# Twelve-layer latent transformer on one core: the second norm of layer 5 as one factor a token, the last quarter's turn moved behind the first products of nine layers, the last layer's mean by TensorE

## The chip, the cores and the metric

One core of one Trainium2 chip. The kernel is one program of about 71,000 instructions, with one instruction stream for each of TensorE (PE), VectorE (DVE), ScalarE (ACT), GpSimd (POOL) and SyncE (SP, which issues all DMAs). The metric is the device time of one execution in microseconds.

## The reference, cut to what matters

The state `x` is 64 batches x 32 tokens x 128 features (2048 tokens), all in fp32. Twelve layers follow each other, each of the form

```python
x = x + layer(_layernorm(x))      # _layernorm: (x - mean) / sqrt(var + 1e-5), no gain, no offset
```

The layers are: 1 cross attention with mask, 2 linear attention with an MLP, 3 a three-matrix network with binary weights, 4 cross attention with mask, 5 an attention within a batch, 6 a mixture of experts, 7 sigmoid cross attention, 8 latent attention, 9 a grouped expert network, 10 cross attention, 11 an attention with a sparse branch and an MLP, 12 a GRU over the 32 tokens followed by routing and experts. Only in layers 5 and 12 does the arithmetic change. Layer 5 gets `y = _layernorm(x)` and norms it again, this time with a gain and an offset:

```python
h = _layernorm(y) * norm_w + norm_b
q, k, v = split(h @ qkv_w.T + qkv_b)
att = (q @ k.T) * 128 ** -0.5            # no softmax, so no row maxima either
out = y + (att @ v) @ proj_w.T + proj_b  # and then x = x + out
```

Layer 12 starts its GRU from a mean over the tokens of a batch: `h0 = y.mean(axis=1) @ ctx_w.T + ctx_b`.

## The kernel before, in words

**State and tiles.** `X` holds the 2048 tokens as 16 tiles of 128 tokens (partitions) x 128 features, side by side in one 128x2048 buffer; `y` is its norm and `yT` the turned norm (features on the partitions), of the same size. Four tiles are a quarter. `stats`, `moments` (mean and variance of each token) and `rstd` belong to the program and outlive a layer.

**Layers and their order.** Each layer is a class with one method for each engine (`pe`, `act`, `dve`, `pool`, `sp`); each engine works through its method in program order. Between layers stands a barrier: every engine drains, raises `closed` (L3877, L3884, L3891, L3904) and waits until all four have. So a layer starts when its slowest engine is through with the one before. Weights of the next layer are loaded by SP while a layer runs. Nothing is planned at run time; the order is the order of the calls, and waits are on counting semaphores.

**The norm at a layer's head.** A layer norms the first three quarters of the next one while it ends (`next_statistics`, `next_root`, `next_rows`). The last quarter is left to the next layer's head: DVE takes statistics (L103, L106, L109), ACT the square root (L115), DVE the reciprocal and four rows (L121, L124). PE turns all four quarters with 16 transposes (`norm_pe`, L240) into PSUM banks 0 to 3, and ACT copies each bank to `yT` (`norm_act_yT`, L231; L3297 in layer 12, where the copy also reorders the tokens by time). ACT does the square root first and then the four copies. In most layers the first product waits for all four copies, that is for the last quarter. In layer 1 this stays as it is.

**Layer 3** (`L0Ffn`). DVE first does the norm, then maps the three binary matrices from 0/1 to -1/1 (L1715, three instructions), drains, and subtracts the halves of the first (L1718); PE starts its first products (L1676) when all that is done.

**Layers 4 and 10** (`HeadCrossAttention`). PE first folds the last context token (L821 to L828), then does the 16 transposes, then the queries of tile 0 (L880), keys and values of group 0 (L886 to L888), those of group 1, and scores (L899). DVE adds the bias to the queries (L1074, L1076), POOL spreads them over the heads (L1182), DVE builds `wo_heads` (L1022) right behind. The steady state that follows goes by groups of 32 tokens.

**Layer 5** (`L1Attention`). Four groups of 512 tokens go through a pipeline of steps: norm again on DVE (`own_norm`: statistics L279, L282, L285, root on ACT L298, reciprocal L309, rows L312, times gain L303, plus offset L305), transposes (L1800), copy (L1826), queries, keys and values (L1790, L1793), scores (L1782), apply (L1774), projection (L1766). DVE adds three things for each group: projection plus `y` (L1842), plus the offset of the projection (L1844), plus `X` (L1846). Behind the third group stand the rows of three quarters of the next norm. POOL has nothing to do.

**Layer 12** (`L3Ffn`). Behind the four copies DVE sums `yT` over the tokens (L3487) and scales (L3489); PE forms `h0` (L3324); then follow 32 steps of the GRU (L3349) and the experts.

## Time and profile before

| | us |
|---|---|
| median of 3 runs | 3074.31 (3073.43 to 3076.48) |
| the profiled execution | 3070.85 |
| its span, first to last instruction | 3069.1 |
| busy PE, DVE, ACT, POOL | 2812.5, 1702.2, 1319.7, 689.9 |

The chain that ended last is PE for 54% of the span, DVE 7%, POOL 4%, ACT 3%. The layers start at 0, 459.6, 739.7, 838.0, 1113.9, 1160.4, 1266.1, 1354.8, 1500.3, 1586.3, 1854.1 and 2021.4 us of the span. How to read it: every row gives a start or a count, a duration, the engine, the line of the kernel, and what is written from what; the bracket at the end of a row is the idle time of the engine before it and what ended that.

### The profile page before, as it was taken

To read this page: it belongs to the slowest core of one execution; us is meant where nothing else is said; L and a number is where in the kernel's file an instruction comes from. 1 tells how busy PE (TensorE), PEld (TensorE's weight loads), DVE (VectorE), ACT (ScalarE), POOL (GpSimd) and SP (SyncE) were. 2 spreads that over 40 slices of the span, in tenths; PEclk is the share of its full clock that TensorE was granted. 3 is DMA by queue.
4 is the path that set the end of the run, shared out by engine and by line. 5 is a ranking of instruction groups with operands and counts; after the bars stand their busy time and mean duration, and the time that the engine had idled before them with its cause. 6 is when DMAs were issued, how large, how long until landed. Compare 5 with 4: busy or idle time off the path is not lost.

```text
span 3069.1 us, 71179 instructions
## 1 busy us (share of the span) xinstructions
PE 2812.5 (92%) x27569; PEld 1813.6 (59%) x27569; DVE 1702.2 (55%) x5653; ACT 1319.7 (43%) x3579; POOL 689.9 (22%) x1524
## 2 busy tenths in 40 slices
PE   8999998997999978999689997779999999999898
PEld 7888885554567755665457775534444444444465
DVE  6777777674166677558746765842233232232544
ACT  4655555542278842348538883411111121121222
POOL 2444440000067720024116661100000000000000
PEclk9999999998999988888779998989999999999999
DMA  5111110000021100230011113040000000000000
GB/s 133 49 47 47 49 31 8 2 3 5 12 55 48 48 25 3 67 106 2 5 40 43 39 29 142 2 136 1 1 1 1 1 1 1 1 1 1 1 1 14
DMA packets 125910, 92.28 MB, mean 30 GB/s; under 512 B 41027, under 2 KB 122566, under 8 KB 124230
## 3 DMA queue, kind: packets, MB, share of 16 engines
q1 hardware_dynamic: 125574, 87.74, 10.1%
q8 instruction: 219, 3.59, 0.5%
q14 instruction: 117, 0.96, 0.1%
HBM read 84.02 MB, written 3.67 MB: 29 GB/s over the span
## 4 chain that ended last, share of the span: by engine, by line
PE 54%; DVE 7%; issue 5%; POOL 4%; ACT 3%; DVEq 2%; POOLq 2%; ACTq 0%
PE banks L3349 24%; POOL probs L1208 3%; PE banks L918 2%; PE banks L3768 2%; PE banks L3759 2%; PE banks L3757 2%; PE banks L1682 2%; PE banks L899 1%; POOLq L1209 1%; PE banks L927 1%; PE banks L886 1%; PE banks L3404 1%; PE banks L2301 1%; PE banks L3359 1%; PE banks L1924 1%
## 5 line engine op out<-in xcount | busy, mean ns | idle before, releaser
L1008 ACT ACTIVATE probs<-probs,nbias 128x257 f32<-128x257 f32 x512 | 254.7, 507 | 0.0
L1208 POOL TENSOR_SCALAR probs<-probs,rinv 128x257 f32<-128x257 f32 x512 | 237.9, 485 | 29.3 <-DVE rinv L1102 25.6
L3349 PE MATMUL banks<-Wz,hT 128*64 128x256 f32 x2048 | 226.4, 379 | 0.0
L3349 PE MATMUL banks<-Wn,hT 128*64 128x512 f32 x1024 | 225.4, 593 | 0.0
L3349 PE MATMUL banks<-Wr,hT 128*64 128x512 f32 x1024 | 225.2, 592 | 0.0
L3618 POOL COPY rb<-hT 128x512 f32<-128x512 f32 x32 | 35.8, 1119 | 801.3 <-ACT hT L3424 777.0
L3349 PEld LDWEIGHTS banks<-Wz,hT 128*64 128x64 f32 x2048 | 147.0, 137 | 87.7 <-issue 18.3
L3592 DVE TENSOR_TENSOR pr<-hb,banks 128x512 f32<-128x512 f32 x32 | 22.0, 688 | 298.3 <-PE banks L3404 298.3
L712 POOL TENSOR_SCALAR probs<-probs,rinv 128x257 f32<-128x257 f32 x256 | 120.6, 485 | 201.3 <-DVE rinv L652 200.7
L3349 PEld LDWEIGHTS banks<-Wr,hT 128*64 128x64 f32 x1024 | 73.5, 137 | 132.6 <-issue 128.0
L3349 PEld LDWEIGHTS banks<-Wn,hT 128*64 128x64 f32 x1024 | 70.9, 137 | 129.5 <-issue 129.5
L918 PE MATMUL banks<-ident,probs 128*128 128x128 f32 x1024 | 140.7, 281 | 4.1 <-POOLq L1209 2.7
L3479 ACT ACTIVATE sq<-banks 128x512 f32<-128x512 f32 x32 | 19.1, 598 | 284.0 <-DVE pr L3592 284.0
L485 PE MATMUL banks<-kvT,qh 128*128 128x257 f32 x512 | 133.8, 384 | 1.0 <-ACT bo_rows L545 1.0
L568 ACT ACTIVATE probs<-banks,nbias 128x257 f32<-128x257 f32 x256 | 119.6, 474 | 34.6 <-DVE rinv L652 31.1
L918 PEld LDWEIGHTS banks<-ident,probs 128*128 128x128 f32 x1024 | 110.3, 141 | 31.0 <-issue 22.7
L640 DVE SCALAR_TENSOR_TENSOR banks<-banks,r_all,keep 128x257 f32<-128x257 f32 x256 | 113.2, 485 | 12.2 <-PE banks L485 8.1
L643 DVE CUSTOM_DVE_ANT_0 banks<-banks,fill 128x257 f32<-128x257 f32 x256 | 105.3, 447 | 15.0 <-issue 0.5
L1091 DVE CUSTOM_DVE_ANT_0 probs<-banks,fill 128x257 f32<-128x257 f32 x256 | 93.2, 421 | 21.5 <-PE banks L907 21.5
L1091 DVE CUSTOM_DVE_ANT_0 probs<-banks,zeros 128x257 f32<-128x257 f32 x256 | 93.2, 421 | 15.1 <-PE banks L899 15.1
L1008 ACT ACTIVATION_READ_ACCUMULATOR probs<-probs,nbias 128x1 f32 x512 | 99.7, 195 | 0.0
L3457 ACT ACTIVATE h<-banks 128x512 f32<-128x512 f32 x72 | 42.7, 598 | 132.1 <-PE banks L3757 132.1
(632 smaller groups left out, 6399.2 us busy)
## 6 DMA issues: line engine op xcount, KB each, us to landing
kvT<-in_ctx_T SPq DMA_DIRECT2D x192, 128.5 KB
kv<-in_ctx SPq DMA_DIRECT2D x64, 128.0 KB
kv<-in_ctx SPq DMA_DIRECT2D x32, 256.0 KB
W<-in_L_ffn_W_T SPq DMA_DIRECT2D x2, 2048.0 KB
Wr<-in_L_ffn_w_hh_T SPq DMA_DIRECT2D x1, 4096.0 KB
Wn<-in_L_ffn_w_hh_T SPq DMA_DIRECT2D x1, 4096.0 KB
Wz<-in_L_ffn_w_hh_T SPq DMA_DIRECT2D x1, 4096.0 KB
v_last<-v_last SPq DMA_DIRECT2D x192, 8.0 KB, 1.6
```

The source lines that it names most:

```text
L485: e.matmul(self.bank[self.S_BANK + n][:, 0:CTX], self.qh[t % 2][:, (4 * b + n) * P:(4 * b + n + 1) * P], self.kvT[b][:, :], start=True, st ...
L568: e.activation(self.probs[v][:, j * CTX:(j + 1) * CTX], self.bank[self.S_BANK + 2 * z + j][:, 0:CTX], ACT.Exp, bias=self.nbias[v][:, j:j + ...
L640: e.scalar_tensor_tensor(s[j], s[j], self.r_all[t % 2][:, r:r + 1], keep, ALU.add, ALU.mult)
L643: e.tensor_tensor_reduce(s[j], s[j], fill, 1.0, -3.0e38, ALU.add, ALU.max, top[j])
L712: i = e.tensor_scalar(s, s, self.rinv[v][:, j:j + 1], 1.0, ALU.mult, ALU.mult)
L918: i = e.transpose(self.bank[self.T_BANK + c][:, r * P:(r + 1) * P], probs[:, r * CTX + c * P:r * CTX + (c + 1) * P], self.prog.ident[:, :])
L1008: i = e.activation(s, s, ACT.Exp, bias=self.nbias[v][:, r:r + 1], scale=self.scale, accum_out=self.rows_sum[v][:, r:r + 1])
L1091: i = e.tensor_tensor_reduce(self.probs[v][:, r * CTX:(r + 1) * CTX], self.bank[r][:, 0:CTX], add, 1.0, -3.0e38, ALU.add, ALU.max, self.ma ...
L1208: e.tensor_scalar(s, s, self.rinv[v][:, r:r + 1], 1.0, ALU.mult, ALU.mult)
L1682: i = e.matmul(self.bank[2 + c % 2][:, :], self.W[1][:, k * 512 + c * P:k * 512 + (c + 1) * P], h0[:, k * R4:(k + 1) * R4], start=k == 0, ...
L3349: mm = e.matmul(self.bank[b][hf * BATCH:(hf + 1) * BATCH, 0:n], lhs, rhs, start=start, stop=stop, tile_position=(0, hf * BATCH))
L3757: e.matmul(self.bank[c][:, :], self.gate[:, o:o + P], yT, start=True, stop=True).then_inc(self.gate_mm.up(), 1)
```

## The change

- `norm_pe` and `norm_act_yT` take a list of quarters, and a stage may name the banks of the turns (`TURN_BANKS`).
- In layers 2 to 4 and 6 to 12 PE turns three quarters (one in layers 4, 10 and 11, the next two a little later), starts the first products that need only those, and turns the last quarter behind some of them. ACT copies one to three quarters ahead of the square root.
- Layer 3: the signs come ahead of the norm on DVE, and the first products wait for the first matrix alone; the root moves to round 1, the last quarter's turn to round 2.
- Layers 4 and 10: DVE takes the first queries between statistics and rows; POOL no longer waits for the rows.
- Layer 5: the second norm becomes one factor a token (`again`). The mean of `y` is zero and its variance is var * rstd^2, so the factor is 1 / sqrt(var * rstd^2 + 1e-5), from numbers that the first norm left. The gain is folded into the weights (`qkvG`), the offset into the biases (three small products into bank 7). POOL scales the rows and adds `y` and the projection's offset to `X`; DVE is left with one sum for each group, and with one quarter of the next rows for each group from the second on.
- Layer 7: DVE takes statistics, then fills `of_batch`, then the rows, and only then copies the folded matrices (`fold_ready`); ACT runs a square root on a constant at the head, which loads its table.
- Layer 8, 9, 11: order at the head. In layer 11 the sigmoid of `lam` moves behind the first projections and two quarters.
- Layer 12: PE forms the sum over the tokens with 16 products of a tile of `y` with a 128x4 matrix of zeros and ones that POOL builds (`of_row`); DVE only scales.

```diff
@@ layer 2: L0Attention, pe and act
-        self.norm_pe(e)
+        self.norm_pe(e, (0, 1, 2))
         self.weights_wait(e)
         for c in range(self.C):
             self.features(e, 0, c)
+            if c == 1:
+                self.norm_pe(e, (3,))
...
+        self.norm_act_yT(e, (0, 1))
         self.norm_act_std(e)
-        self.norm_act_yT(e)
+        self.norm_act_yT(e, (2,))
...
@@ layer 3: L0Ffn, pe, act, dve
-        self.norm_pe(e)
+        self.norm_pe(e, (0, 1, 2))
         self.signs_ready.wait_ge(e, 1)
-        self.n_yT.wait_ge(e, 4)
...
+            if r == 2:
+                self.norm_pe(e, (3,))
             for c in range(FC):
+                self.n_yT.wait_ge(e, max(r, c % 2) + 1)
...
-        self.norm_act_std(e)
-        self.norm_act_yT(e)
-        self.signs_ready.wait_ge(e, 1)
+        self.norm_act_yT(e, (0, 1, 2))
+        self.weights_wait(e)
...
+            if r == 1:
+                self.norm_act_std(e)
+            if r == 2:
+                self.signs_ready.wait_ge(e, 3)
+                self.norm_act_yT(e, (3,))
@@ layers 4 and 10: HeadCrossAttention, pe
-        p.constants_made.wait_ge(e, 1)
+        self.norm_pe(e, (0,))
         self.weights_wait(e)
...
+        self.norm_pe(e, (1, 2))
+        self.x_free = None
+        self.n_yT.wait_ge(e, 1)
+        self.prep_act.wait_ge(e, 1)
+        self.project(e, 0)
...
+        self.keys_values(e, 0)
+        self.norm_pe(e, (3,))
         self.n_yT.wait_ge(e, 4)
-        self.project(e, 0)
-        self.keys_values(e, 0)
@@ layer 5: L1Attention
+    def again_dve(self, e, n):
+        p, at = self.prog, self.tiles_again(n)      # n = 0: tiles 0 to 11, n = 1: tiles 12 to 15
+        r, rstd = self.again[:, at], p.rstd[:, at]
+        var = p.moments[:, 2 * at.start:2 * at.stop].rearrange("p (t two) -> p t two", two=2)[:, :, 1]
+        e.tensor_tensor(r, rstd, rstd, ALU.mult)
+        e.drain()
+        e.tensor_tensor(r, r, var, ALU.mult)
+        e.drain()
+        e.tensor_scalar(r, r, 1e-5, None, ALU.add).then_inc(self.again_var.up(), 1)
...
-                y, x, t1 = p.y[:, g * R4:(g + 1) * R4], p.X[:, g * R4:(g + 1) * R4], self.t1[g % 2]
-                e.tensor_tensor(t1[:, :], self.bank[6][:, :], y, ALU.add).then_inc(self.y_added.up(), 1)
-                e.drain()
-                e.tensor_tensor(four(t1), four(t1), row4(self.bp), ALU.add)
-                e.drain()
-                e.tensor_tensor(x, x, t1[:, :], ALU.add)
+                x = p.X[:, g * R4:(g + 1) * R4]
+                self.x_offset.wait_ge(e, g + 1)
+                e.tensor_tensor(x, self.bank[6][:, :], x, ALU.add).then_inc(self.x_done.up(), 1)
                 e.drain()
                 if g < 3:
                     self.next_statistics(e, g)
-                if g == 2:
-                    for q in range(3):
-                        self.next_rows(e, q)
+                if g:
+                    self.next_rows(e, g - 1)
...
+    def pool(self, e):
+        p = self.prog
+        self.weights_wait(e)
+        e.tensor_scalar(self.qkvG[:, :], self.qkvT[:, :], self.gw[:, 0:1], 1.0, ALU.mult, ALU.mult).then_inc(self.gained.up(), 1)
+        self.norm_again(e, 0)
+        self.norm_again(e, 1)
+        p.rowed.wait_ge(e, NT * (self.index + 1))
+        for g in range(self.GROUPS):
+            if 2 <= g + 1 < self.GROUPS:
+                self.norm_again(e, g + 1)
+            x, y_bp = p.X[:, g * R4:(g + 1) * R4], self.y_bp[g % 2]
+            e.tensor_tensor(four(y_bp), p.y[:, g * R4:(g + 1) * R4].rearrange("p (t d) -> p t d", d=P), row4(self.bp), ALU.add)
+            e.drain()
+            e.tensor_tensor(x, x, y_bp[:, :], ALU.add).then_inc(self.x_offset.up(), 1)
+
+    def norm_again(self, e, g):
+        self.again_ready.wait_ge(e, 1 + g // 3)
+        self.h_turned.wait_ge(e, g - 1)
+        for t in range(4 * g, 4 * g + 4):
+            s = t % 4
+            i = e.tensor_scalar(self.hn[g % 2][:, s * P:(s + 1) * P], self.prog.y[:, t * P:(t + 1) * P], self.again[:, t:t + 1], 1.0, ALU.mult, ALU.mult)
+        i.then_inc(self.hn_ready.up(), 1)
@@ layer 6: L1Ffn, pe (layer 7 has the same with cg in place of Wr)
+            if t == 12:
+                self.norm_pe(e, (3,))
+            self.n_yT.wait_ge(e, t // 4 + 1)
             i = e.matmul(bank[6][:, t * E:(t + 1) * E], yT[:, t * P:(t + 1) * P], self.Wr[:, :], start=True, stop=True)
@@ layer 7: L2CrossAttention, act
+        e.activation(self.warm[:, :], self.prog.ones[:, 0:1], ACT.Sqrt)
+        self.norm_act_yT(e, (0, 1))
         self.norm_act_std(e)
-        self.norm_act_yT(e)
+        self.norm_act_yT(e, (2, 3))
@@ layer 12: L3Ffn, pe and dve
-        self.norm_pe(e)
+        self.norm_pe(e, (0, 1, 2))
+        self.of_row_made.wait_ge(e, 1)
+        for t in range(NT):
+            if t == 12:
+                self.norm_pe(e, (3,))
+            i = e.matmul(bank[4][:, BPT * t:BPT * (t + 1)], p.y[:, t * P:(t + 1) * P], self.of_row[:, :], start=True, stop=True)
+        i.then_inc(self.mean_mm.up(), 1)
...
-        self.n_yT.wait_ge(e, 4)
-        e.tensor_reduce(self.mean[:, :], p.yT[:, :].rearrange("p (t b) -> p b t", b=BATCH), AX.X, ALU.add)
-        e.drain()
-        e.tensor_scalar(self.mean[:, :], self.mean[:, :], 1.0 / SEQ, None, ALU.mult).then_inc(self.mean_ready.up(), 1)
+        self.mean_mm.wait_ge(e, 1)
+        e.tensor_scalar(self.mean[:, :], bank[4][:, 0:BATCH], 1.0 / SEQ, None, ALU.mult).then_inc(self.mean_ready.up(), 1)
```

## Rows read from the trace of the kernel before

**Rows 1.** Stretches by layer: us, busy PE, PEld, DVE, ACT, POOL, granted clock, DMA share.
```profile
1113.90:1160.40 46.50, 29.33 (x160) 22.59 (x160) 40.10 (x145) 11.17 (x24) 0.04 (x1) 0.76 0.14 34
2021.40:3069.10 1047.70, 1023.38 (x6274) 487.99 (x6274) 358.27 (x732) 195.88 (x364) 40.26 (x55) 0.99 0.04 12
```
**Rows 2.** Groups by line in layer 5: shapes, count, busy us, mean ns, idle.
```profile
L312 DVE TENSOR_SCALAR hn<-y,mv,rstd 128x128 f32<-128x128 f32 x16 | 4.5, 342 | 0.3
L305 DVE TENSOR_TENSOR hn<-hn,gb 128x512 f32<-128x512 f32 x4 | 2.8, 692 | 0.3
```
**Rows 3.** Groups by line of POOL, whole span.
```profile
L1208 POOL TENSOR_SCALAR probs<-probs,rinv 128x257 f32<-128x257 f32 x512 | 237.9, 485 | 29.3 <-DVE rinv L1102 25.6 <-issue 2.5
L1182 POOL TENSOR_TENSOR qbd<-q,of_group 128x512 f32<-128x512 f32 x32 | 37.2, 1163 | 85.8 <-DVE q L1076 51.0 <-DVE q L1074 34.8
L1186 POOL COPY kT<-k_last 128x1 f32<-128x1 f32 x128 | 24.0, 188 | 12.4 <-PE banks L907 7.2 <-PE banks L899 5.2
L1642 POOL TENSOR_TENSOR y_bo<-y,bo 128x512 f32<-128x512 f32 x4 | 5.1, 1266 | 128.9 <-DVE s L1629 126.1 <-DVE y L124 2.8
```
**Rows 4.** Timeline of layer 5's head and of the next layer's first instruction: start, us, what.
```profile
1121.10 3.50 PE L1790 MATMUL banks<-hT,qkvT 128*128 128x512 f32 x4 [1.01 <-ACT hT L1826]
...
1160.43 4.17 PE L240 MATMUL banks<-ident,y 128*128 128x128 f32 x16 [5.83 <-DVEq L3891]
```
**Rows 5.** Timeline of POOL and DVE at layer 4's head.
```profile
844.88 2.28 DVE L1022 TENSOR_TENSOR wo_heads<-wo,head_mask 128x2048 f32<-128x2048 f32 x1
845.04 3.01 POOL L1182 TENSOR_TENSOR qbd<-q,of_group 128x512 f32<-128x512 f32 x1 [0.42 <-DVE q L1074]
```
**Rows 6.** Chain of waits at layer 3's head: start, us, what.
```profile
742.96 2.07 DVE W L1715 x3
745.18 0.69 DVE W L1718
745.96 6.75 PE banks L1676 x8
```
**Rows 7.** Timeline of layer 2's head.
```profile
459.59 1.53 PE L240 MATMUL banks<-ident,y 128*128 128x128 f32 x12 [0.99 <-POOLq L3904]
465.19 1.28 ACT L1510 ACT_TABLE_LOAD   x1 [1.32 <-PE banks L1360]
467.28 0.76 DVE L1589 TENSOR_SCALAR banks<-banks,bq 128x512 f32<-128x512 f32 x1 [4.35 <-ACT ex L1510]
```
**Rows 8.** Chain of waits in the heads of layers 4 and 10.
```profile
850.12 1.17 PE banks L899 x8
...
1594.01 2.95 POOL qbd L1182
1597.23 0.71 PE banks L899 x8
```
**Rows 9.** Chain of waits at the heads of layers 6, 7, 8 and 9.
```profile
1165.28 7.01 PE banks L1906 x32
...
1274.29 6.96 PE banks L2094 x32
...
1360.72 0.57 PE banks L2469 x2
...
1504.62 1.14 PE banks L3090 x2
```
**Rows 10.** Chain of waits at the heads of layers 11 and 12.
```profile
1863.53 1.89 PE banks L2301 x64
...
2023.37 3.53 ACT yT L3297 x4
2026.92 3.57 DVE mean L3487
2030.91 1.99 PE banks L3324 x4
```
**Rows 11.** The span and its mean granted clock.
```profile
core 0: 3069.1 us, clock 0.950
```

More of the change, by code:

```diff
@@ L199, in norm_dve, with own_quarters, norm_dve_statistics, norm_dve_rows @@
     def norm_dve(self, e):
-        quarters = range(3 if self.index else 0, 4)
+        self.norm_dve_statistics(e)
+        self.norm_dve_rows(e)
+    def own_quarters(self):
+        return range(3 if self.index else 0, 4)
+    def norm_dve_statistics(self, e):
         self.prog.x_loaded.wait_ge(e, 1)
-        for q in quarters:
+        for q in self.own_quarters():
             self.prog.norm_statistics(e, self.index, q)
-        for q in quarters:
+    def norm_dve_rows(self, e):
+        for q in self.own_quarters():
             self.prog.norm_rows(e, self.index, q)
@@ L225, in next_rows, with norm_act_yT, norm_pe @@
             self.prog.norm_rows(e, self.index + 1, q)
-    def norm_act_yT(self, e):
+    def norm_act_yT(self, e, quarters=range(4)):
         p = self.prog
-        for q in range(4):
+        for q in quarters:
             self.n_turned.wait_ge(e, q + 1)
-            e.copy(p.yT[:, q * 512:(q + 1) * 512], p.bank[q][:, :]).then_inc(self.n_yT.up(), 1)
-    def norm_pe(self, e):
+            e.copy(p.yT[:, q * 512:(q + 1) * 512], p.bank[self.TURN_BANKS[q]][:, :]).then_inc(self.n_yT.up(), 1)
+    def norm_pe(self, e, quarters=range(4)):
         p = self.prog
         p.constants_made.wait_ge(e, 1)
-        for q in range(4):
+        for q in quarters:
             for r in range(4):
@@ L1742, in __init__ @@
         self.bv, self.bp = self.broadcast_row("bv", w["qkv_b"][2 * P:3 * P]), self.broadcast_row("bp", w["proj_b"])
[L1743 removed]
+        self.gw, self.gb = self.columns("gw", w["norm_w"]), self.columns("gb", w["norm_b"])
         self.end_of_weights()
[L1745 removed]
+        self.same, self.qkvG = sb("same_batch", [P, P]), sb("qkvG", [P, 3 * P])
+        self.again = sb("again", [P, NT])
         two = lambda n: [sb(n, [P, R4]) for _ in range(2)]
[L1747 removed]
+        self.hn, self.hT, self.v, self.att, self.oT, self.y_bp, self.qT, self.kT = (two(n) for n in ("hn", "hT", "v", "att", "oT", "y_bp", "qT", "kT"))
         self.norm_signals(turned=False)
[L1749 removed]
+        self.gained, self.offset_mm, self.offset_ready = sig("gained", 1), sig("offset_mm", 1), sig("offset_ready", 1)
+        self.again_var, self.again_std, self.again_ready = sig("again_var", 2), sig("again_std", 2), sig("again_ready", 2)
         self.hn_ready, self.h_turned, self.hT_ready = sig("hn_ready", N), sig("h_turned", N), sig("hT_ready", N)
@@ L1759, in pe @@
         self.weights_wait(e)
+        for n in range(2):
+            e.matmul(bank[7][:, n:n + 1], self.qkvT[:, n * P:(n + 1) * P], self.gb[:, 0:1], start=True, stop=True)
+        e.matmul(bank[7][:, P:2 * P], self.gb[:, 0:1].to_broadcast([P, P]), self.qkvT[:, 2 * P:3 * P], start=True, stop=True).then_inc(self.offset_mm.up(), 1)
+        self.gained.wait_ge(e, 1)
         for step in range(N + 4):
@@ L1804, in act @@
         N = self.GROUPS
-        self.norm.act(e)
+        self.again_act(e, 0)
         self.norm_act_std(e)
+        self.again_act(e, 1)
+        self.offset_ready.wait_ge(e, 1)
         for step in range(N + 4):
@@ L1826, in act, with tiles_again, again_act, again_inverse @@
                 e.copy(self.hT[g % 2][:, :], self.bank[0][:, :]).then_inc(self.hT_ready.up(), 1)
-                if g + 1 < N:
-                    self.norm.act(e)
+    def tiles_again(self, n):
+        return slice(12 * n, 12 + 4 * n)
+    def again_act(self, e, n):
+        r = self.again[:, self.tiles_again(n)]
+        self.again_var.wait_ge(e, n + 1)
+        e.activation(r, r, ACT.Sqrt).then_inc(self.again_std.up(), 1)
+    def again_dve(self, e, n):
[7 more added lines that the diff above has]
+        e.tensor_scalar(r, r, 1e-5, None, ALU.add).then_inc(self.again_var.up(), 1)
+    def again_inverse(self, e, n):
+        r = self.again[:, self.tiles_again(n)]
+        self.again_std.wait_ge(e, n + 1)
+        e.reciprocal(r, r).then_inc(self.again_ready.up(), 1)
     def dve(self, e):
         p, N = self.prog, self.GROUPS
+        self.again_dve(e, 0)
+        self.norm_dve_statistics(e)
+        self.again_inverse(e, 0)
+        self.norm_dve_rows(e)
+        e.drain()
+        self.again_dve(e, 1)
         self.weights_wait(e)
-        self.own_norm(e, 0)
-        self.norm_dve(e)
+        self.offset_mm.wait_ge(e, 1)
+        e.tensor_tensor(self.bqk[:, :], self.bank[7][:, 0:2], self.bqk[:, :], ALU.add).then_inc(self.offset_ready.up(), 1)
+        e.tensor_tensor(self.bv[:, :], self.bank[7][:, P:2 * P], self.bv[:, :], ALU.add)
+        self.again_inverse(e, 1)
         same_batch(e, self.same, P ** -0.5)
@@ L3290, in tiles, with norm_act_yT @@
         return self.prog.X[t * BATCH:(t + 1) * BATCH, :].rearrange("b (j d) -> b j d", d=P)
-    def norm_act_yT(self, e):
+    def norm_act_yT(self, e, quarters=range(4)):
         p = self.prog
         by_time = p.yT[:, :].rearrange("p (t b) -> p b t", b=BATCH)
-        for q in range(4):
+        for q in quarters:
             self.n_turned.wait_ge(e, q + 1)
@@ L3606, in pool @@
         E = self.E
+        e.memset(self.of_row[:, :], 0.0)
+        e.drain()
+        for b in range(BPT):
+            e.memset(self.of_row[b * SEQ:(b + 1) * SEQ, b:b + 1], 1.0)
+        e.drain().then_inc(self.of_row_made.up(), 1)
         s3 = self.same[:, :].rearrange("p (b e) -> p b e", e=E)
```

132 lines of the change are left out of this document (75 added, 57 removed).

## The prediction, made before the change was run

> **What bounds the kernel now.** I read four views, in this order. First the stretches by layer: the last layer is PE at 1023.4 of 1047.7 us and near full clock, so nothing there moves but its head; layer 5 takes 46.5 us, in which DVE is busy 40.1 and PE 29.3, at a mean clock of 0.76 [rows 1]. Second the groups by line, to see what DVE does in layer 5: most of it is the second norm and the three sums [rows 2], and POOL does nothing. Third the chain of waits around the start of each layer: it passes through the last quarter's norm, its four turns and its copy before the first product may start. Fourth the timeline there, for what each engine is late with. Eleven heads and one DVE-bound layer are thus what the change can shorten; each head is costed as the difference in the start of the first piece of work that the rest of the layer follows.
>
> **Layer 5.** DVE loses, for each of 4 groups, four rows of 0.28 apart (their group mean of 0.34 counts the overlap), gain and offset at 0.69 each [rows 2], and statistics, which the shared ones price at about 1.4, plus two of three sums of the same shape at 0.69: 4 x (1.1 + 1.4 + 1.4 + 1.4 + 0.2) = 22 us. It gains some 3 us of small instructions. POOL gets 4 x 4 rows of 128x128 (between the 0.19 of a 1-column copy and the 0.485 of 257 columns [rows 3]; I take 0.33, near the middle as the width is) and 8 sums of 1.27 [rows 3]: 5.3 + 10.1 = 15.4 us beside the others. DVE is then at about 21 of 40 us and the bound goes to the order of PE and, at the end, of DVE again. I followed it: the factor of tiles 0 to 11 is ready about 2.5 us in (three small steps on DVE, a root, statistics of the last quarter queued between, a reciprocal), POOL's first four rows at 1118.0, turns at low clock until 1118.9. ACT's first copy waits for DVE's bias (`offset_ready`, 1119.05; behind DVE's last quarter and `again_dve(1)`), so the first queries start at 1119.8, against 1121.10 [rows 4]. From there a step is five or six blocks of PE (turns 0.55, queries and keys 1.9, values 1.0, scores, apply, projection 0.95 each: about 5.5 us) where it was a DVE step. Steps 2 to 5 start at 1124.4, 1128.8, 1134.1, 1139.7. In steps 5 and 6 DVE has sum 0.7, statistics 1.6 and rows 1.3 ahead of what PE needs next; the last sum ends at 1149.4 and the rows of the third quarter at 1150.7. The next layer began at 1160.43 [rows 4]: **-9.6**. Bounds: -11.5 if the low clock at the end does not reach the last products, -7 if the steps keep a gap of 0.5 us each as before.
>
> [...]
>
> **Layer 3.** Now the first products start at 745.96, after DVE's norm, 2.07 of signs and 0.69 of difference [rows 6]. Signs first: matrix 0 is 1024 of 3584 columns, 0.6, plus 0.69 and a drain, ready at 741.1, hidden behind 12 turns that at low clock end at 742.2. So -3.75. The four turns come back in round 2 (0.13 each at full clock [rows 7], 0.55), their copy (0.6) behind PE's first product. DVE's last quarter now waits for ACT's root in round 1; behind it on DVE is only the first sum to `X`, needed two rounds later. **-3.2**; from -2.5, if the low clock that now lasts from before this head to past 750 lasts just as long (8 products took 6.75, at full clock they would take 3.6), to -6.
>
> **Layer 2.** ACT begins with quarters 0 and 1 and does the root 0.3 later. First feature product at 461.15, so the table load of 1.28 can run at 462.3 instead of 465.19, and DVE's first feature work at 464.4 instead of 467.28 [rows 7]. The copy of the last quarter (0.58) falls into ACT's exponentials behind the second chunk; DVE's period of 2.03 hides half of it. **-2.5** (-2.0 to -2.9).
>
> **Layers 4 and 10.** Scores of group 0 started at 850.12 and 1597.23 [rows 8]. In layer 10 the queries come 2.1 earlier (project before the last quarter), and POOL's 2.95 [rows 8] no longer starts together with `wo_heads` but 1.3 ahead of it; then PE's own order decides: keys of group 0, four turns, a wait for the copy of quarter 3, which ACT does behind the copies of group 0 (until 1594.4), keys of group 1, scores at 1595.75. **-1.5**. In layer 4 POOL still maps the mask until 844.6 and meets `wo_heads`, the same order on PE gives 848.75 instead of 850.12, and the part that lies in the low clock gives some back: **-1.0**. Together -1.2 to -3.5.
>
> **Layers 6 to 9 and 11.** Layer 6: 32 passes of 0.22 take 7.01 [rows 9] at low clock; now 24 of them start at 1163.0, then four turns 0.9, a wait of 0.8 for the copy, 8 passes 1.75: end 1171.6 instead of 1172.29, **-0.7**. Layer 7: the table load (1.28, as [rows 7]) goes under the turns, but the root is behind two copies (1270.1), the rows end at 1271.7, and DVE copies the folded matrices only then, so `fold_ready` is at 1272.8, where PE has been waiting since 1270.5. 24 passes, turns, copy, 8 passes of the 6.96 [rows 9] end at 1281.5 instead of 1281.25: **+0.3**. Layer 8: the first queries start when the three small products are through, 1358.95 instead of 1360.52 (the chain counts it from 1360.72 [rows 9]); the four turns return in step 2 at 0.9: **-0.65**. ACT stands waiting for that turn with the values of tile 0 behind it; they are needed 0.3 later, so this is close. Layer 9: first logits 1504.62 [rows 9], now 1502.3, but DVE is free only at 1503.65: -2.2, and four turns at 0.9 come back between pick and logits: **-1.2**. Layer 11: the projections start 4 us earlier, but ACT now has to take them, load the sigmoid's table (1.28) and copy the last quarter at 63.0, and `values` waits for that copy: 1863.1 instead of 1863.53 [rows 10], **-0.3**. These five: between 0 and -6.
>
> **Layer 12.** The four copies of about 1 us (3.53) and the sum of 3.57 leave the path to `h0`, which started at 2030.91 [rows 10]. In their place: turns of three quarters to 2023.85, 24 passes for the sum, four turns, 8 passes, a scale of 0.2. A pass has no row of its own; the nearest are those of layers 6 and 7, 0.22 at low clock [rows 9], and 0.13 for a 128x128 turn at full clock [rows 7]. All low: 2032.2, +1.4. All full: 2028.8, -2.1. This stretch changes its clock in the middle; I take **-0.5**. The copies remain, but are needed only by the first step. The four DMAs of the head and SP's queue are passed by none of this: the rows that `X` waits for are made as before.
>
> **Sum**: -9.6 -3.2 -2.5 -1.5 -1.0 -0.7 +0.3 -0.65 -1.2 -0.3 -0.5 = **-20.85**. The profiled execution had 3070.85 (span 3069.1 and 1.75 around it), so 3050.0; the median of the runs lay 3.5 above it, so **3053.5**.
>
> **Rivals.**
> A, *POOL is held up in layer 5*. For: 3.01 against 1.16 [rows 3, 5]. [...] If all POOL work there took 2.6 times as long, 40 us, the last `x_offset` would come near 1160 and layer 5 would win nothing: 3063. [...]
> B, *the heads give nothing that lasts*: the layer's steady state was waiting for something else than its head (in layers 4 and 10 POOL's 0.485 x 4 for each group [rows 3], in layers 6 and 12 the passes at low clock). Only layer 5 remains: 3064. Against: the chain of waits runs through every one of these heads.
> C, *the low clock ends sooner*: PE has fewer gaps at the heads. The 6.75 of layer 3 could shorten by 2.5, the 7.01 and 6.96 [rows 6, 9] by half of it in part, layer 12 by 1.6: together about 8 more, 3045. Against: the passes of layers 6 and 7 kept PE busy for 7 us and did not end it.
> D, the other side: *more of the chip at low clock*. The mean clock is 0.950 over 3069.1 us [rows 11], which is 2 x 0.05 x 3069 = 307 us at the lower of two levels. A further microsecond there costs at most 0.5 of PE-bound work. It takes 42 us more (a mean of 0.943) to cancel the sum, and 54 (0.941) to be slower by 6: 3081. It decides in the layers where PE now has small products behind long waits (5 to 9). For: layer 5 gets PE work in shorter blocks. Against: it would have to spread far beyond the heads.
> E, *the change doesn't do what it says*: turning the mean over to PE costs more than DVE's 3.57, up to +1.4. Alone it only moves the sum by 2 and is inside the range.
>
> **Chances.** Forecast 0.63, A 0.08, B 0.12, C 0.13, D 0.02, something that leaves it within 0.2% 0.02. The bounds of the parts, added as independent, give -20.85 with about 5 either way; towards A and B the range goes to their times, towards C to its own: 3044 to 3064. A measurement of this kernel can tell about 0.2% (6 us). Faster by more than that: 0.94; within: 0.04; slower: 0.02.
>
> **What would show it.** Layer 5 near 37 us long, DVE busy about 21, POOL about 15 with sums near 1.27, the step of PE near 5.5 us; L1676 starting 2.5 us behind layer 3's start; the first scores of layers 4 and 10 about 10.7 and 9.5 us behind theirs; layer 7 not shorter at its head, with PE waiting for DVE before L2094; `h0` 8 to 10 us behind the start of layer 12. Wrong if POOL's rows or sums in layer 5 take 2 us and more, if the heads' gains are not found again where the layer ends, or if the mean clock leaves 0.94 to 0.96.

## The result, and the profile after

The changed kernel took 3047.06 us (median of 4 runs, 3040.35 to 3049.31) against 3073.87 (4 runs, 3069.47 to 3076.48): ratio 0.9911, 95% interval 0.9891 to 0.9930, 27 us less. Forecast: 3053.5, range 3044 to 3064. Three later comparisons, with the same kernel (experiment 3) and with two that differ in one detail (experiments 5 and 6), gave 0.9928 (0.9899 to 0.9956), 0.9921 (0.9903 to 0.9938) and 0.9925 (0.9904 to 0.9945): 22 to 24 us less. The other four variants of the whole change (experiments 4, 7, 8 and 10) lie between 0.9916 and 0.9936, 20 to 26 us less. The working sum was 20.85.

The two profiled executions are only 21.5 apart (3070.85 and 3049.31; spans 3069.1 and 3047.6). First the stretches by layer of the changed kernel, the view of [rows 1] (us, busy PE, PEld, DVE, ACT, POOL with counts, granted clock, DMA share, GB/s):

```profile
0.00:464.93 464.93, 441.86 (x3268) 385.35 (x3268) 344.98 (x1282) 264.21 (x799) 186.35 (x446) 1.00 0.22 59
744.80:838.55 93.75, 89.69 (x304) 47.47 (x304) 16.62 (x65) 24.70 (x40) 0.00 (x0) 0.97 0.02 4
1111.52:1150.15 38.63, 30.36 (x167) 23.99 (x167) 21.53 (x83) 10.99 (x22) 16.19 (x25) 0.77 0.17 42
1566.87:1837.13 270.26, 252.73 (x3168) 191.52 (x3168) 178.27 (x816) 215.34 (x734) 164.03 (x432) 0.95 0.16 42
2003.12:3047.60 1044.48, 1025.55 (x6306) 491.83 (x6306) 354.69 (x731) 195.79 (x364) 40.55 (x60) 0.99 0.04 12
```

Layer 1, which no edit touches, is 464.93 us here and was 459.6. The 5.3 us are lost between its 14th and its 33rd us: PE's products on `bias` start at 14.52 instead of 14.27, those on `wo,wv` at 32.43 instead of 26.99. The view gives a clock of 1.00 for all of this stretch in this execution, but its first clock record stands only at 30.4 us, so the clock ahead of that was not measured. PE's small products on `bias`, x16 each, in the groups by line of the first 30 us, before and then after:

```profile
L391 PE MATMUL banks<-bias,wk 128*128 128x2 f32 x16 | 3.1, 265 | 0.0
```

```profile
L397 PE MATMUL banks<-bias,wk 128*128 128x2 f32 x16 | 4.5, 353 | 0.0
```

Layer 1 lay between 459.2 and 464.9 in all 13 profiles of this study, old and new, so this is a matter of the execution. That the clock was low there is an estimate from these durations (353 ns for 265) and from no record of the clock. In layers 2 to 12 this pair of profiles differs by 26.9 us.

Layer 5 answers to [rows 2, 3, 4]. Its groups by line (busy us, mean ns, idle before):

```profile
L1942 POOL TENSOR_SCALAR hn<-y,again 128x128 f32<-128x128 f32 x16 | 5.6, 372 | 1.8 <-DVE again L1882 1.7
L1933 POOL TENSOR_TENSOR y_bp<-y,bp 128x512 f32<-128x512 f32 x4 | 5.1, 1268 | 0.0
L1935 POOL TENSOR_TENSOR X<-X,y_bp 128x512 f32<-128x512 f32 x4 | 5.1, 1266 | 0.6
L1905 DVE TENSOR_TENSOR X<-banks,X 128x512 f32<-128x512 f32 x4 | 2.8, 689 | 1.5 <-PE banks L1797 1.5
L1915 DVE TENSOR_TENSOR att<-banks,same_batch 128x512 f32<-128x512 f32 x4 | 2.8, 688 | 2.2 <-PE banks L1813 2.2
```

POOL's sums take 1.27 as forecast, its rows 0.35 to 0.37 (forecast 0.33), POOL is busy 16.2 (15.4), DVE 21.5 (21). Rival A is out: no sum or row on POOL was stretched. PE's first queries start 6.1 us behind the layer's start (forecast 5.9), and those of the next groups 6.5, 4.9 and 5.7 us after each other (forecast about 5.5). The end of layer 5 in the timeline of the changed kernel, DVE and PE:

```profile
1141.29 1.12 DVE L124 TENSOR_SCALAR y<-X,moments,rstd 128x128 f32<-128x128 f32 x4 [0.43 <-issue]
1142.32 0.69 DVE L1915 TENSOR_TENSOR att<-banks,same_batch 128x512 f32<-128x512 f32 x1
1143.06 2.04 PE L1805 MATMUL banks<-att,v 128*128 128x128 f32 x8 [1.94 <-DVE att L1915]
1145.78 2.08 PE L1797 MATMUL banks<-projT,oT 128*128 128x128 f32 x8 [0.67 <-ACT oT L1845]
1147.89 0.69 DVE L1905 TENSOR_TENSOR X<-banks,X 128x512 f32<-128x512 f32 x1 [0.66 <-PE banks L1797]
1148.93 1.11 DVE L124 TENSOR_SCALAR y<-X,moments,rstd 128x128 f32<-128x128 f32 x4
1150.15 0.48 PE L246 MATMUL banks<-ident,y 128*128 128x128 f32 x1 [2.29 <-DVEq L4000]
```

PE waits 1.94 for the mask of the last group, which stands behind a quarter of rows on DVE, and then runs its last 16 instructions at low clock (2.04 and 2.08 for eight, at a granted clock of 0.51 and 0.50; 1.16 each at 1.00 in experiment 1). Those 1.8 us are about what layer 5 (38.63) has over the forecast 37.

The heads, each mark counted from the start of its layer (forecast in brackets): L3 first product 2.6 (2.5), was 6.3 [rows 6]; L2 first feature work of DVE 4.75 (4.8), was 7.7 [rows 7]; L4 scores 10.1 (10.7), was 12.0; L10 scores 10.95 (9.5), was 10.95 too [rows 8]; L6 routing's end 8.7 (11.2), was 11.8; L7 sum's end 13.8 (15.4), was 15.1; L8 first queries 3.9 (4.1), was 5.7 [rows 9]; L11 values 10.5 (9.0), was 9.4; L9 first logits 2.6 (2.0), was 4.3 [rows 9]; L12 `h0` 7.5 (9.0), was 9.45 [rows 10]. In the timeline, layers 3, 7 and 12:

```profile
747.41 1.06 PE L1694 MATMUL banks<-yT,W 128*128 128x512 f32 x1
...
1257.55 3.83 PE L2172 MATMUL banks<-cg,yT 128*128 128x1 f32 x24 [1.89 <-DVEq L2279]
...
2005.73 3.21 PE L3424 MATMUL banks<-of_row,y 128*128 128x4 f32 x24
2009.27 0.95 PE L3424 MATMUL banks<-of_row,y 128*128 128x4 f32 x8
2010.63 1.97 PE L3429 MATMUL banks<-ctxT,mean 128*64 128x512 f32 x4 [0.41 <-DVE mean L3593]
```

Layer 7 shows the wait of PE for DVE's folded matrices (1.89), as forecast. The 24 passes of layer 12 took 3.21, 0.13 each.

### The profile page after: what moved, and what is told of

It is laid out like the page before. It is cut to its first block, busy times and chain, and to the rows that moved or that the text cites. A ratio compares the mean times of both kernels' runs of the same rounds, so it can differ in the third digit from the quotient of the medians.

```text
span 3047.6 us, 71215 instructions
## 1 busy us (share of the span) xinstructions
PE 2814.9 (92%) x27607; PEld 1820.8 (60%) x27607; DVE 1681.1 (55%) x5590; ACT 1318.8 (43%) x3578; POOL 702.0 (23%) x1554
## 3 DMA queue, kind: packets, MB, share of 16 engines
q1 hardware_dynamic: 125574, 87.61, 10.2%
## 4 chain that ended last, share of the span: by engine, by line
PE 51%; issue 8%; DVE 7%; POOL 4%; ACT 2%; POOLq 2%; DVEq 2%; ACTq 0%
PE banks L3454 24%; POOL probs L1220 3%; PE banks L927 2%; PE banks L3877 2%; PE banks L3868 2%; PE banks L3866 2%; PE banks L908 1%; POOLq L1221 1%; PE banks L936 1%; PE banks L895 1%; PE banks L3509 1%; PE banks L3464 1%; PE banks L2382 1%; PE banks L1998 1%; PE banks L246 1%
```

## The experiments

The clock's records of the 13 profiles hold two values alone, 0.50 and 1.00. In the kernel before, eight products of 128x512 took 6.75 us at 0.50 and 32 of them 13.90 at 1.00, 0.84 and 0.43 each, so by an estimate from these a low-clock us costs about 0.5 of PE-bound work:

```profile
745.96 6.75 PE L1676 MATMUL banks<-yT,W 128*128 128x512 f32 x8 [2.47 <-DVEq L1719]
752.55 13.90 PE L1682 MATMUL banks<-h,W 128*128 128x512 f32 x32
```

```profile
746.00:752.00 6.00, 6.00 (x7) 2.37 (x8) 0.00 (x0) 1.89 (x3) 0.00 (x0) 0.50 0.01 3
753.00:766.00 13.00, 13.00 (x32) 5.68 (x30) 0.00 (x0) 2.50 (x4) 0.00 (x0) 1.00 0.00 0
```

A layer's low-clock time is worked out as 2 x (1 - mean granted clock) x its length, with the clock's unrounded record. It moves between executions of one kernel, so a layer is read as a pair: length / low-clock us.

**1. Layer 5 alone.** The kernel before, with the class `L1Attention` of the changed one.

> Only layer 5 is changed; the other eleven heads are as before. If the sum of the prediction holds, layer 5 is 38 to 39 us long here too (46.5 before) and the time is 8 to 10 us under before, with nothing after layer 5 moved except by the clock. Rival B (all that the change wins is layer 5) expects the full difference here: 20 us and more under before. Rival A (POOL held up) expects sums over 2 us on POOL and less than 3 us won. The extra that the runs showed over the forecast (27 against 21) should not be here if it belongs to the heads, and 5 us of either sign may come from low clock in the first 30 us, which no edit touches.

3059.26 us (10 runs), ratio 0.9959 (0.9940 to 0.9978), 13 us less by the ratio. Layer 5:

```profile
1118.19:1154.83 36.64, 28.24 (x167) 22.06 (x167) 21.42 (x83) 11.12 (x22) 16.16 (x25) 0.86 0.17 44
```

36.64 / 10.5: the forecast's 37, and its -9.6 is -9.8 here (46.4 in the first profile of the kernel before, counted alike). It is below the 38 to 39 expected for this run, and the time, by its interval 7 to 18 us less, holds both the 8 to 10 us of the sum and the 13 measured, but not the 20 and more of rival B as it is put there. Its last attention products are not at low clock (1.00 from 1149.1 to 1150.4), which is the difference from the 38.63 above; DVE's order is the same:

```profile
1148.45 0.68 DVE L1897 TENSOR_TENSOR att<-banks,same_batch 128x512 f32<-128x512 f32 x1
1149.19 1.16 PE L1787 MATMUL banks<-att,v 128*128 128x128 f32 x8 [1.72 <-DVE att L1897]
```

**2. The heads alone.** The changed kernel, with `L1Attention` of the kernel before.

> Everything is as in the changed kernel, but layer 5 is the one of before (46.5 us). Forecast: 11 us under before, with the marks of the heads as in the changed kernel (first product of layer 3 2.6 us behind its start instead of 6.3, first DVE feature work of layer 2 at 4.75 instead of 7.7). Rival B expects the marks to move but the layers to keep their length: 0 to 2 us under before. Rival C (low clock ends sooner with the new heads) expects 15 us and more under before, with layers 4, 6 and 8 again 3 to 5 us shorter.

3060.17 us (10 runs), ratio 0.9949 (0.9926 to 0.9971), 16 us less (9 to 23). Layer 5 is 46.02 / 18.7, with DVE busy 40.07, and the marks of layers 2 and 3 are those of the changed kernel (4.77 and 2.62). Experiments 1 and 2 add up to 28, with intervals of 6 and 7 either way: both halves are real, and rival B, under which this one would be at 0 to 2, is out for the heads as a whole. The time does not part the forecast (11) from rival C (15 and more): layers 4, 6 and 8 were 2.8, 2.4 and 6.0 us shorter than in the first profile of the kernel before, where rival C had 3 to 5 for each.

**3. The changed kernel again.**

> The changed kernel a second time, for the spread of one kernel's executions. If the low clock is a matter of the execution and not of the edits, the same layers (1, 4, 6, 8, 10) come out 2 to 5 us longer or shorter than in the first profile, in step with their low-clock time at about 0.5 us for each us; if it is a matter of the new order of work, each layer repeats its length and its low-clock time within 1 us. Time 3040 to 3050 either way.

3050.32 (3041.34 to 3056.78, 6 runs), just above the 3040 to 3050 expected; ratio 0.9928. Layer 4 came out 275.3 / 12.5 against 273.0 / 5.9, layer 6 102.5 / 13.7 against 100.9 / 10.0, layer 7 89.9 / 28.4 against 87.7 / 21.6; that is 0.32 to 0.42 us for each low-clock us, where 0.5 was expected; layers 3, 5, 8, 10 and 12 repeated within 0.7. So part of the clock's pattern is the execution's, but layer 10 had 24.5 us of low clock twice.

**4. DVE's order at the end of layer 5.**

```diff
-                if g:
-                    self.next_rows(e, g - 1)
+                if g == 3:
+                    self.next_rows(e, 1)
+                    self.next_rows(e, 2)
...          behind the mask of the last group:
+                if g == 3:
+                    self.next_rows(e, 0)
```

> The changed kernel, but in layer 5 DVE does the mask of the last group ahead of the rows of the first quarter, and the rows of the other two quarters behind the last sum. In the changed kernel PE waited 1.94 us for that mask, behind 1.0 us of rows. If the end of layer 5 hangs on this order, layer 5 becomes 1.5 to 2.5 us shorter (36.5 us) and PE's wait ahead of the last attention products falls below 1 us. If it hangs on the amount of DVE work at the end (two quarters of rows, 1.1 us each and a reciprocal), the rows only move behind the last sum and the layer keeps 38.6 within 0.5.

3050.51 us, ratio 0.9916 (0.9886 to 0.9945). PE's wait ahead of the last attention products fell from 1.94 to 0.31, and layer 5 is 36.38 / 12.5. By the number this is the first reading: 2.2 less than in the changed kernel's profile. But it is only 0.3 less than in experiment 1, which has the changed kernel's order and the better clock, and the same order came to 36.6 in three more profiles (experiments 6, 7 and 9, with 10 us of low clock). The timeline of the end of this layer:

```profile
1135.87 1.16 PE L1805 MATMUL banks<-att,v 128*128 128x128 f32 x8 [0.31 <-DVE att L1916]
1139.29 0.69 DVE L1905 TENSOR_TENSOR X<-banks,X 128x512 f32<-128x512 f32 x1
1140.33 1.11 DVE L124 TENSOR_SCALAR y<-X,moments,rstd 128x128 f32<-128x128 f32 x4
1141.61 1.11 DVE L124 TENSOR_SCALAR y<-X,moments,rstd 128x128 f32<-128x128 f32 x4
```

The last sum starts 32.9 us behind the layer's start, against 34.4 in experiment 7, but two quarters of rows stand behind it instead of one (1.3 each with the reciprocal). So nearly all of the gain went into the rows behind the last sum, as the second reading says, and the 38.6 that it was tied to was the clock's. The 2.5 us more at low clock may hide up to 0.8 of gain, at the price of 0.31 found below; that is not parted here.

**5. Folding without GpSimd.** Gain, rows and sums of layer 5 all on DVE: `pool` is gone, DVE calls `norm_again` for the next group and the two sums of this one at the end of each step.

> The changed kernel, but in layer 5 DVE does all that GpSimd was given (gain on the projection, 16 rows, 8 sums). It tells the folding from the move. If the folding did most of it (statistics, gain and offset gone: 4 x (1.4 + 1.4) = 11 us of DVE's 40), layer 5 is 38 to 39 us here too. If the move to GpSimd was needed, DVE is busy 21.5 + 16 x 0.28 + 8 x 0.69 + 0.5 = 32 us, the last sum waits for it and layer 5 comes out between the two, 40 to 42 us. If GpSimd and DVE get in each other's way in the changed kernel (rival A), this one is the faster.

3046.85 us, ratio 0.9921 (0.9903 to 0.9938). Layer 5:

```profile
1106.46:1143.24 36.78, 28.24 (x166) 22.07 (x166) 29.26 (x108) 11.11 (x22) 0.00 (x0) 0.85 0.18 44
```

36.78 / 10.7 against 36.64 / 10.5: the move to GpSimd is worth nothing. DVE is busy 29.3 of 36.8. PE's wait for the rows of the second norm (us in total, times, the longest), in the kernel before and then here:

```profile
PE banks L1800 <- DVE hn L305: 8.7, 3, 6.0
```

```profile
PE banks L1831 <- DVE hn L1942: 2.0, 1, 2.0
```

What is left is one wait of 2.0 for the first rows (2.4 with GpSimd) and one of 1.6 for the last mask (1.9). DVE's 10.8 us less than before match the 11 that the expectation gives statistics, gain and offset. But two of the three sums also stand elsewhere now: they are made ahead of the projection and not behind it. The folding and this new order together did it all; no run has the one without the other.

**6. The mean of layer 12 by DVE**, as before (the reduction of `yT` in place of the 32 passes on `of_row`).

> The changed kernel, with the mean of layer 12 by DVE as before. h0's products start 9.4 to 9.7 us behind the start of the layer, as in both profiles of the old order. With TensorE they started at 7.5 where the clock was full for part of the head and at 10.6 where it was low throughout. Theory of the prediction (the passes cost by the clock): layer 12 is the same within 1.5 us either way. Rival E (TensorE's mean is dearer): layer 12 shorter here by 1 us and more in every state.

3049.21 us, ratio 0.9925. Layer 12 is 1047.68 / 23.7, as in the two profiles of the kernel before (1047.67 / 23.7 and 1047.64 / 23.6); the old head in experiment 1 gave 1046.41 / 25.8. With TensorE's mean nine profiles gave 1044.5 / 20.5 (twice) up to 1049.5 / 32.4. The head with DVE's mean, and then the passes in experiment 2, where the whole head was at low clock:

```profile
2006.83 3.57 DVE L3588 TENSOR_REDUCE mean<-yT 128x64 f32<-128x2048 f32 x1 [1.47 <-ACT yT L3396]
2010.82 1.98 PE L3424 MATMUL banks<-ctxT,mean 128*64 128x512 f32 x4 [5.07 <-DVE mean L3590]
```

```profile
2011.33 5.05 PE L3377 MATMUL banks<-of_row,y 128*128 128x4 f32 x23
2017.13 1.71 PE L3377 MATMUL banks<-of_row,y 128*128 128x4 f32 x8
```

`h0` started 9.98 us behind the layer's start, not 9.4 to 9.7: the fourth copy ends 5.96 behind it instead of 5.43, since the root now stands behind two copies. 0.22 a pass at a granted clock of 0.50 (experiment 2, 5.05 for 23), 0.13 at a mean of 0.85 (the changed kernel, 3.21 for 24): the prediction's two prices, and its two ends (`h0` at 10.6 and 7.5, against 9.45 with DVE's mean in the kernel before: +1.15 and -1.95). Which of them comes was the clock's choice; low throughout in seven of the nine profiles. For the mark, rival E is right for those seven, and within its 1.4. As put in the expectation (shorter here in every state) it is not: the two profiles with the full clock for part of the head are 3.2 us shorter than this run.

**7. The old head in layer 10 alone.**

> The changed kernel, with the head of layer 10 alone in its old order (all turns, then the first queries; copies of the turns behind bo_rows). In three of the four profiles with the new head layer 10 was 270.3 to 270.7 us long with 24.5 us of low clock, in two with the old head 267.8 with 11.8. If the new order of this head brings the low clock, layer 10 is 267.8 us again with some 12 us of low clock. If the low clock comes from where layer 9 ends and not from the head, it stays near 24 us and the layer is 271 to 272 us long, since the gain of the head (1.5) is gone as well.

3049.03 us, ratio 0.9926 (0.9909 to 0.9942). Layer 10 with its neighbour ahead:

```profile
1475.91:1561.87 85.96, 64.45 (x872) 47.73 (x873) 39.30 (x116) 34.31 (x108) 0.00 (x0) 0.68 0.02 5
1561.87:1832.84 270.97, 252.16 (x3168) 191.25 (x3168) 177.48 (x815) 215.46 (x734) 166.14 (x432) 0.96 0.16 42
```

270.97 / 21.8, scores at 11.99 instead of 10.95. The low clock is not the new head's doing. Nor is it the change's: see experiment 11.

**8. Three further edits**: in layer 5 the rows of the next layer's first three quarters on GpSimd (DVE keeps the reciprocals), in layer 7 the copies of the folded matrices ahead of the rows, in layer 11 the last quarter's turns and copy ahead of the sigmoid.

> The changed kernel with three further edits. Layer 5: mask of the last group ahead, and the rows of the next layer's first three quarters by GpSimd, which had nothing to do at the end; DVE keeps the reciprocals. If the tail hangs on DVE's amount of work, layer 5 ends 2 to 2.5 us earlier than in l5_order (34 us); if GpSimd's rows (4 x 0.35) are as late as DVE's were, no gain. Layer 7: copies of the folded matrices ahead of the last rows: the first 24 passes start 5.2 us behind the layer's start instead of 6.5. Layer 11: the last quarter's turns and copy ahead of the sigmoid's table load: the first values start 9.2 us behind instead of 10.5. Together -4 to -5 us if head starts last until the end of their layers, 0 if not.

3050.58 us, ratio 0.9936 (0.9917 to 0.9955): no gain. Layer 5 is 38.92 / 15.0, longer than in experiment 4, though its last projection ended at the same place (32.3 us behind the start). POOL's groups by line in that layer, and then in experiment 10:

```profile
L1942 POOL TENSOR_SCALAR y<-X,moments,rstd 128x128 f32<-128x128 f32 x12 | 9.3, 787 | 10.8 <-DVE rstd L1949 10.8
L1956 POOL TENSOR_SCALAR hn<-y,again 128x128 f32<-128x128 f32 x16 | 5.6, 373 | 1.7 <-DVE again L1883 1.7
```

```profile
L1944 POOL TENSOR_SCALAR y<-X,moments,rstd 128x128 f32<-128x128 f32 x4 | 3.1, 792 | 10.7 <-DVE rstd L1951 10.7
```

A row with two scalars from SBUF took POOL 0.79 here, twice the 0.37 of one with a scalar and a constant; my expectation of 0.35 was the price of the other kind. The 12 rows end 5.5 us behind DVE's last work, and each took 0.78 to 0.80, beside that work and behind it, so the price is not one of contention. Layer 11 is the sharper lesson: its values started at 8.86 instead of 10.52, and it was 167.67 / 44.8 long, against 167.64 / 44.8 in experiment 4. The layer does not hang on that mark.

**9. Extra products in layer 9**, whose results nobody reads.

```diff
+                for _ in range(2):   # behind each logit product
+                    e.matmul(bank[7][:, :], self.Wc[:, :], p.yT[:, 0:R4], start=True, stop=True)
...
+                e.matmul(bank[3][:, 0:P], self.Wc[:, :], p.yT[:, 0:P], start=True, stop=True)   # behind inner_pe
```

> The changed kernel, and in layer 9 TensorE also does products whose results nobody reads: two of 128x512 behind each logit product, one of 128x128 behind each of the 16 blocks of inner products. In seven profiles of the changed order layer 9 was 85.3 to 86.0 us long with 51 to 55 of its us at low clock. If the low clock there is a matter of how little TensorE does between its waits, its low-clock time falls (below 40 us) and the layer gets shorter by up to 0.33 us for each us of it, less what the added products delay. If it is not, the low-clock time stays at 51 to 55 us and the layer is 0 to 4 us longer.

```profile
1483.77:1576.29 92.52, 80.01 (x921) 57.32 (x921) 39.42 (x116) 34.44 (x108) 0.00 (x0) 0.70 0.02 5
```

3062.31 us, ratio 0.9966 (0.9951 to 0.9981). PE went from 64 to 80 us busy and the low-clock time stayed at 55.0 us; the layer became 6.6 us longer, more than the 4 expected. More products of this size and place did not buy the clock back.

**10. The tail shared out**: GpSimd one quarter of rows, DVE two; layer 7 as in experiment 8.

> The changed kernel, with the tail of layer 5 shared out by what three_more showed (a GpSimd row with two scalars from SBUF took 0.78 us, DVE's four rows 1.1 to 1.3): GpSimd does the rows of the first quarter alone, DVE those of the other two behind the last sum; and layer 7 copies its folded matrices first. Layer 5 is 35.5 to 36 us long (36.4 to 36.8 in the profiles with full clock at its end), if DVE's work is the tail; 36.4 and more if GpSimd's 3.1 us hold up DVE's rows, which wait for them. Layer 7 0.5 us shorter at equal clock. In the total that is under what can be measured.

Layer 5 is 35.88 / 12.0, the shortest of all, 0.5 under experiment 4, as expected. Layer 7 is 87.29 / 22.4, 0.4 under the changed kernel's 87.70 / 21.6. The time is 3051.84 (3046.57 to 3059.20, 5 runs), ratio 0.9921 (0.9894 to 0.9948): not to be told from the changed kernel's. No version here beats it by what can be measured.

**11. The kernel before again.**

> The kernel before a second time. If the change lowers the low-clock time as a whole (283 to 306 us in layers 2 to 12 in the profiles of the changed heads, 306.5 and 307.2 with the old ones), this one shows 303 us and more again, with layer 8 above 70 us of it and layer 4 above 16. If the difference is one of executions, it lies anywhere in 283 to 310.

3078.75 us (8 runs), ratio to its own other runs 1.0017 (1.0001 to 1.0034): the interval of one kernel against itself misses 1 by a little, so the intervals here are somewhat narrow. Low clock in layers 2 to 12: 303.1 us, with 72.6 in layer 8 and 15.6 in layer 4 (just under the 16 expected). Old heads: 306.5, 303.1, 307.2; new heads, ten profiles: 283.0 to 327.1, mean 298.9. The total is thus not shown to have changed. Layer 10:

```profile
1581.61:1852.81 271.20, 252.02 (x3168) 191.05 (x3168) 177.76 (x816) 215.61 (x734) 166.77 (x432) 0.96 0.16 42
```

271.20 / 22.0 with nothing changed: the 267.8 / 11.8 of the first profile was a lucky one. One profile does not give a layer's length.

## Why the prediction was right, step by step

Means over the profiles; the third column is the plain difference, the fourth the difference at equal low-clock time, from a least-squares fit of one length for each version of a layer and one price for a low-clock us (0.31, uncertainty 0.02; the layers' own about 0.5):

```
layer   old length/low   new length/low   plain   equal clock   forecast
 2      279.5 / 16.6     279.6 / 23.6      0.0      -2.1         -2.5
 3       97.8 / 10.7      93.3 /  4.7     -4.6      -2.7         -3.2
 4      275.3 / 16.5     273.5 /  7.4     -1.8      +1.1         -1.0
 5       46.3 / 18.9      37.3 / 12.8     -9.0      -7.0         -9.6
 6      105.2 / 16.2     103.0 / 14.3     -2.2      -1.6         -0.7
 7       89.5 / 22.3      88.9 / 24.6     -0.6      -1.3         +0.3
 8      144.3 / 72.7     141.9 / 66.8     -2.4      -0.6         -0.65
 9       86.8 / 56.1      85.7 / 53.5     -1.1      -0.3         -1.2
10      268.9 / 15.2     269.2 / 21.5     +0.3      -1.7         -1.5
11      167.3 / 38.8     166.8 / 42.4     -0.5      -1.7         -0.3
12     1047.2 / 24.4    1047.9 / 26.9     +0.7      -0.1         -0.5
sum                                      -21.2     -18.1        -20.85
```

(Old: 3 profiles; new: 6 to 10, those whose layer is as in the changed kernel. The old heads of experiments 6 and 7 are not in; with them the plain differences of layers 12 and 10 are +0.6 and -0.2.) Both uncertainties are lower bounds: fitted for each layer alone, the price runs from 0.19 (layer 9) to 0.47 (layer 12), and four of the profiles repeat layers 7 and 8 within 0.1 us, so they are not independent draws.

- **The sum** of -20.85 holds: -21.2 plain, -18.1 at equal clock (about 1.6 either way if the layers' errors are independent). That the plain sum comes within 0.4 is partly luck: single terms are off by up to 2.5 (layer 2), on both sides, and cancel. The first pair of profiles showed 26.9 because the changed kernel's had 16.5 us less low clock (290.0 against 306.5; at 0.31 that is 5.1). Layer 1's 5.3 took the same amount back.
- **Layer 5**: the term and its mechanism are right (DVE was the bound; 36.6 to 38.6 for 37). But part of the step's account is wrong: it counted the sums that went to POOL and the rows there as work that had to leave DVE. Experiment 5 shows that it was enough to remove statistics, gain and offset and to make two of the sums earlier; the remaining DVE work fits beside PE. The price that the prediction feared (rival A) and the gain it claimed for that part are both nil.
- **Layer 2**: the plain 0.0 hides the gain, since the new profiles had 7.0 us more of low clock there. Two profiles, experiment 7 (new head) and experiment 11 (old), have the same four low stretches in this layer, each 2.8 us earlier in the new one:

```profile
462.66:737.81 275.15, 235.22 (x4864) 152.77 (x4864) 189.72 (x526) 125.19 (x192) 10.39 (x9) 0.98 0.02 4
459.47:737.45 277.98, 235.90 (x4864) 152.83 (x4864) 189.60 (x526) 125.64 (x192) 10.37 (x9) 0.98 0.02 4
```

  So the edit is worth 2.8 here, where the step had 2.5. Whether the new head brings the added low clock is not shown: ten profiles have 12.7 to 29.8 us of it, the three old ones 12.7 to 18.9.
- **Layer 3** is the clearest head: a mark 3.7 us earlier, and a layer 4.6 shorter, 1.9 of it by less low clock in all ten profiles. That is one part of rival C that exists: [rows 6] had its eight products at low clock, now they end 7.3 to 8.0 us behind the start instead of 11.7 to 13.1.
- **Layers 6, 8 and 9**: the first queries of layer 8 came as forecast (3.9 for 4.1) and its term holds at equal clock (-0.6 for -0.65), while the plain -2.4 is mostly the clock's. Layer 6 gained more than the step had (-1.6 at equal clock for -0.7), with the routing's end at 8.7 to 11.3, by the clock (forecast 11.2). In layer 9 the logits came 1.7 to 2.1 earlier, but at equal clock -0.3 is left of -1.2; why is open.
- **Layer 7** had the wrong sign. The wait for `fold_ready` came as forecast, but the length fell by 0.6 (1.3 at equal clock). The mark was 13.5 to 16.0, by the clock; its two ends straddle the old 15.1, so the forecast +0.3 is inside that spread. Why the mean lies below is open.
- **Layer 11**: the mark failed. `values` started 10.5 behind the layer's start (9.75 to 10.7 in the nine new profiles), not 9.0; the old ones had 9.4, 9.4 and 10.9. It waits for the last quarter's copy, and ACT's queue of copies, table load, sigmoid and two projections took until 1847.02, one us longer than the prediction had it, with PE's first projections at low clock. Experiment 8 shows that it does not matter, and that the head was the wrong place to read this layer's change. What shortened it is not shown. That the plain -0.5 lies near the term's -0.3 is luck: the mark that the term was read from moved the other way.
- **Layer 10**: -1.5 was right at equal clock (-1.7), and hidden in the first pair of profiles, because their clocks differ. With the head mostly at low clock the scores came at 11.9 and 12.0 in the old order (experiments 11 and 7) and at 10.95 in the new; with less of it at 10.95 to 11.05 and at 10.0 (experiments 4 and 8). The mark moves by 0.95 to 1.0, where the step had 1.5.
- **Layer 4**: the fit's +1.1 should not be believed: old and new hardly overlap in low-clock time (15.6 to 17.2 against 5.9 to 12.5), so the fit cannot part the edit from the clock. The plain -1.8 is what can be said. The clock's part is at the head that was changed: by the clock's record, the first 30 us of the layer have 10.2 to 13.7 us of low clock in the old profiles and 3.4 in nine of the ten new ones. That is the other part of rival C that exists.
- **Layer 12 and rival E**: a mechanism right at both ends and a value of -0.5 that hides them; the mean of the nine profiles is +0.7, -0.1 at equal clock. The end that was worked out as +1.4 is +1.3 by its own numbers.
- **Rival D** did not happen as a whole, yet it is what blurs every term: at 0.31 us for each low-clock us, the 44 us between the luckiest and the unluckiest of the new profiles are 14 us.
- **Rival A** did not happen. The sum had POOL's work in layer 5 at the undisturbed prices, with 3.01 against 1.16 [rows 3, 5] as the warning. All eight sums of POOL took 1.26 to 1.28, also those beside which DVE worked on a bank (1.27 at 1122.23, with DVE's 0.69 at 1122.99). In the one longer stretch of the new layer 5 where both work from SBUF, DVE's four rows took 1.53 instead of 1.11, and POOL's 0.35 each as elsewhere. The price of this move was 0.4 us, paid by DVE alone; why it was so much less than in [rows 5] is not shown. The rows, from the timeline of the changed kernel:

```profile
1114.03 2.80 POOL L1942 TENSOR_SCALAR hn<-y,again 128x128 f32<-128x128 f32 x8 [1.71 <-DVE again L1882]
1114.34 1.53 DVE L124 TENSOR_SCALAR y<-X,moments,rstd 128x128 f32<-128x128 f32 x4
```

## What to carry to other kernels

Ask of each edit in a bundle whether it is needed once the others are in: here the algebra (one factor instead of a second norm), with two sums made earlier, did the work, and the move to a free engine gained nothing. A mark that moves at a layer's head is only a gain if the layer's end moves, so state both in a forecast. Where the clock of the executions drifts, compare layers by pairs of length and low-clock time over several profiles, of the old kernel too, before believing a difference of a few us.

## What was not expected of the hardware

- POOL's row with two per-partition scalars took 0.79 us on 128x128, the one with a scalar and a constant 0.37 (experiments 8 and 10).
- A low-clock us cost 0.31 us of this kernel by the fit, less than the 0.5 estimated from 0.84 and 0.43 us for a product of 128x512 at a clock of 0.50 and 1.00. The author's guess is that other engines bound part of it; no run shows it.
- In the first 30 us of an execution the same small products took 265 ns in one profile and 353 in another, both at a stated clock of 1.00; in the second the clock's record begins only at 30.4 us, behind them.
- With 16 us more of PE work in layer 9 (80 us busy instead of 64) its low-clock time was 55.0 us, against 51 to 55 in seven profiles without (experiment 9).
